# Cross-attention on one core: V's two halves as one stationary operand, and a context that is summed on VectorE and split on GpSimd

## The reference

```
q = jnp.einsum('bsd,dhk->bshk', query_input, Wq)
k = jnp.einsum('bsd,dhk->bshk', key_input, Wk)
v = jnp.einsum('bsd,dhk->bshk', value_input, Wv)
q = q * depth ** (-0.5)
logits = jnp.einsum('bthk,bfhk->bhft', k, q)
weights = jax.nn.softmax(logits, axis=-1)
ctx = jnp.einsum('bhft,bthk->bfhk', weights, v)
return jnp.einsum('bfhk,hkd->bfd', ctx, Wo)
```

## Time and profile before

| | |
|---|---|
| median of 3 runs | 3175.88 us (3175.04 to 3178.29) |
| span of the profiled execution, first to last instruction | 3171.4 us |
| PE busy | 3088.7 us, 97% of the span |
| PEld busy | 2900.2 us, 91% |
| DVE busy | 2256.1 us, 71% |
| ACT busy | 2142.4 us, 68% |
| POOL busy | 1581.9 us, 50% |
| mean granted TensorE clock | 0.990 |

### The profile page before, as it was taken

One profiled execution on the slowest core, in us unless ns is written; L12 is line 12 of the kernel. 1 busy time (PEld: TensorE's weight loads), 2 busy tenths in 40 slices (PEclk: granted clock), 3 DMA queues, 4 the chain that ended last, 5 costly groups with the idle time before them and its releaser, 6 DMA issues. The chain is left out here.

```text
span 3171.4 us, 78666 instructions
## 1 busy us (share of the span) xinstructions
PE 3088.7 (97%) x22624; PEld 2900.2 (91%) x22624; DVE 2256.1 (71%) x6566; ACT 2142.4 (68%) x6930; POOL 1581.9 (50%) x2904
## 2 busy tenths in 40 slices
PE   6999999999999998999999999999989999999998
PEld 5999999999999987999999999999868888889998
DVE  6777777777877877778877778787745455544665
ACT  6888888888887877787877877777734444442222
POOL 3666766766676765333333333333446666653000
PEclk8999999999999999999999999999989999999999
DMA  6444444444444440121111111111245444533333
GB/s 181 117 120 125 127 125 121 121 120 122 127 111 111 125 143 24 48 64 45 54 55 45 57 55 44 64 45 48 94 118 119 100 98 101 128 56 85 120 124 106
DMA packets 193684, 300.70 MB, mean 95 GB/s; under 512 B 33856, under 2 KB 134080, under 8 KB 192704
## 3 DMA queue, kind: packets, MB, share of 16 engines
q1 hardware_dynamic: 168768, 262.91, 27.8%
q0 software_dynamic: 24576, 33.57, 6.2%
HBM read 116.02 MB, written 67.11 MB: 58 GB/s over the span
## 5 line engine op out<-in xcount | busy, mean ns | idle before, releaser
L964 POOL TENSOR_SCALAR ca_prob<-ca_prob,ca_inverse 128x120 f32<-128x120 f32 x1024 | 354.6, 365 | 632.5 <-DVE ca_inverse L1268 630.5
L665 ACT ACTIVATE sa_prob<-sa_prob,sa_shift 128x128 f32<-128x128 f32 (+1 forms) x1024 | 453.6, 461 | 2.6 <-DVE sa_shift L718 2.6
L1206 ACT ACTIVATE ca_prob<-bank,ca_shift 128x120 f32<-128x120 f32 x1024 | 353.7, 366 | 6.0 <-DVE ca_shift L1262 3.5
L460 POOL TENSOR_SCALAR sa_prob<-sa_prob,sa_inverse 128x128 f32<-128x128 f32 x512 | 198.5, 388 | 234.5 <-DVE sa_inverse L726 220.4
L718 DVE CUSTOM_DVE_ANT_0 sa_prob<-bank,sa_mask 128x128 f32<-128x128 f32 (+1 forms) x1024 | 304.7, 352 | 6.9 <-PE bank L138 2.7
L136 PE MATMUL bank<-sa_ow,sa_y_hi 128*128 128x256 f32 x1024 | 279.6, 304 | 0.0
L136 PE MATMUL bank<-sa_kvT_a,sa_q 128*128 128x128 f32 (+1 forms) x1024 | 251.7, 281 | 17.7 <-DMA sa_q<-sa_q_tile 17.4
L138 PE MATMUL bank<-sa_kvT_b,sa_q 112*128 112x128 f32 (+1 forms) x1024 | 261.6, 281 | 0.0
L749 DVE TENSOR_TENSOR sa_pT_lo<-bank,sa_pT_hi 128x384 fp32r<-128x384 f32 x512 | 258.3, 544 | 1.8 <-ACT sa_pT_hi L650 1.8
L138 PE MATMUL bank<-sa_ow,sa_y_lo 112*128 112x256 f32 x1024 | 258.8, 283 | 0.0
L462 POOL TENSOR_SCALAR sa_prob<-sa_prob,sa_inverse 128x256 f32<-128x256 f32 x512 | 244.9, 478 | 0.0
(11 more groups left out here) (259 smaller groups left out, 12014.1 us busy)
## 6 DMA issues: line engine op xcount, KB each, us to landing
sa_q<-sa_q_tile SPq DMA_DIRECT2D x128, 288.0 KB
sa_q<-sa_q_tile SPq DMA_DIRECT2D x160, 112.0 KB
mid_x2T<-ca_x2T SPq DMA_DIRECT2D x32, 512.0 KB, 3.0
ex_sx<-mid_x2T SPq DMA_DIRECT2D x32, 512.0 KB, 3.3
sa_q<-sa_q_tile SPq DMA_DIRECT2D x304, 32.0 KB, 3.0
sa_xT_raw<-in_xT SPq DMA_DIRECT2D x32, 256.0 KB, 2.8
sa_q<-sa_q_tile SPq DMA_DIRECT2D x32, 256.0 KB
sa_x_res<-in_x SPq DMA_DIRECT2D x32, 256.0 KB, 2.8
```

Source lines behind the costliest of these rows:

```text
L460: pool.tensor_scalar(prob[:, r, hh, 0:P], prob[:, r, hh, 0:P], inverse[:, r, 2 * hh:2 * hh + 1], 1.0, ALU.mult, ALU.mult)
L665: act.activation(prob[:, r, hh, cols], prob[:, r, hh, cols], ACT.Exp, bias=shift[:, r, n:n + 1], scale=-1.0, accum_out=total[:, r, n:n + 1 ...
L964: ins = pool.tensor_scalar(prob[:, r, t, hh], prob[:, r, t, hh], inverse[:, r, n:n + 1], 1.0, ALU.mult, ALU.mult)
L1206: act.activation(prob[:, r, t, hh], SC[g % 2][:, n * S:n * S + S], ACT.Exp, bias=shift[:, r, n:n + 1], accum_out=total[:, r, n:n + 1]).the ...
```

## The change

`v_hi` and `v_lo` become one tensor `v`, in which each head pair has four blocks of 64 columns: high of head 0, low of head 0, low of head 1, high of head 1. A head's stationary operand is its two blocks side by side. It is multiplied by `pT_hi` and by `pT_lo`, two matmuls a head and four a step, into 256 columns of CX for each head, so all 512. The two matmuls give, for head 0, the sum with V's high part on partitions 0 to 63 and with its low part on 64 to 127; for head 1 the other way round. The product of the two low parts is now included.

ACT copies all 512 columns of CX to `cx` (SBUF). DVE adds the half that the copy holds to the half that it reads from the bank, one instruction of 64 partitions a head, into `c`; both halves read the bank at the other half's partitions. GpSimd makes `c_hi` and `c_lo` from `c`. The blocks of zeros in V, their two memsets and the wait for them are gone, and V's split takes one instruction an engine for half a sequence instead of two.

```diff
@@
-    v_hi, v_lo = al.split("v", [S, 2, NP, 3 * DH])
+    al.sb("v_before", [P, PAST_LOW])
+    cx = al.sb("cx", [P, 2, 2 * T])
+    al.sb("v_between", [P, 4 * T - PAST_LOW])
+    v = al.sb("v", [S, 2, NP, 4, DH], F32R)
...
+    c = al.sb("c", [P, 2, T])
@@ gpsimd
-            zeros = [k_hi[0:DH, :, :, S:2 * S], k_lo[0:DH, :, :, S:2 * S], k_hi[DH:P, :, :, 0:S], k_lo[DH:P, :, :, 0:S],
-                     v_hi[:, :, :, DH:2 * DH], v_lo[:, :, :, DH:2 * DH]]
+            zeros = [k_hi[0:DH, :, :, S:2 * S], k_lo[0:DH, :, :, S:2 * S], k_hi[DH:P, :, :, 0:S], k_lo[DH:P, :, :, 0:S]]
...
                 ins.then_inc(p_done, 1)
+            g = m - CL
+            if step_exists(J, g):
+                r = g % RING
+                need(pool, o_mm, upto(J, g - RING))
+                need_alone(pool, csum_done, upto(J, g, 2), spare_pool)
+                pool.tensor_scalar(c_hi[:, r], c[:, g % 2], 1.0, 1.0, ALU.mult, ALU.mult).then_inc(chalf_hi, 1)
+                need(pool, chalf_hi, upto(J, g))
+                pool.tensor_tensor(c_lo[:, r], c[:, g % 2], f32(c_hi[:, r]), ALU.subtract).then_inc(chalf_lo, 1)
@@ tensor
                 need(pe, pTlo_done, upto(J, g))
-                need(pe, cxlo_done, upto(J, g - 1))
+                need(pe, csum_done, upto(J, g - 1, 2))
                 for hh in range(2):
-                    win = slice(hh * DH, hh * DH + 2 * DH)
-                    mm = three(pe, CX[:, 0:T], v_hi[:, b, p, win], v_lo[:, b, p, win], pT_hi[:, r, hh], pT_lo[:, r, hh],
-                               hh == 0, hh == 1)
+                    both = v[:, b, p, 2 * hh:2 * hh + 2].rearrange("s a k -> s (a k)")
+                    out = CX[:, hh * T:(hh + 1) * T]
+                    pe.matmul(out, both, pT_hi[:, r, hh], start=True, stop=False, skip_group_check=True)
+                    mm = pe.matmul(out, both, pT_lo[:, r, hh], start=False, stop=True, skip_group_check=True)
                 mm.then_inc(cx_mm, 1)
...
-                need(pe, cxlo_done, upto(J, g))
+                need(pe, chalf_lo, upto(J, g))
@@ scalar
-                for hh in range(2):
-                    ins = act.activation(v_hi[:, b % 2, n * NP // 2:(n + 1) * NP // 2, hh * 2 * DH:hh * 2 * DH + DH],
-                                         v_bank(J, b, n)[0:S, :].rearrange("s (p h k) -> s p h k", h=2, k=DH)[:, :, hh], ACT.Copy)
-                ins.then_inc(vhi_done, 1)
+                act.activation(v[:, b % 2, n * NP // 2:(n + 1) * NP // 2, 0:4:3],
+                               v_bank(J, b, n)[0:S, :].rearrange("s (p h k) -> s p h k", h=2, k=DH), ACT.Copy).then_inc(vhi_done, 1)
...
-                r = g % RING
                 need(act, cx_mm, upto(J, g))
-                need(act, o_mm, upto(J, g - RING))
-                act.activation(c_hi[:, r], CX[:, 0:T], ACT.Copy).then_inc(cxhi_done, 1)
+                need(act, csum_done, upto(J, g - 2, 2))
+                act.activation(cx[:, g % 2], CX[:], ACT.Copy).then_inc(cxcopy_done, 1)
@@ vector
-                for hh in range(2):
...
-                ins.then_inc(vlo_done, 1)
+                of = v[:, b % 2, n * NP // 2:(n + 1) * NP // 2]
+                dve.tensor_tensor(of[:, :, 1:3], v_bank(J, b, n)[0:S, :].rearrange("s (p h k) -> s p h k", h=2, k=DH),
+                                  f32(of[:, :, 0:4:3]), ALU.subtract).then_inc(vlo_done, 1)
...
-                r = g % RING
-                need(dve, cxhi_done, upto(J, g))
-                dve.tensor_tensor(c_lo[:, r], CX[:, 0:T], f32(c_hi[:, r]), ALU.subtract).then_inc(cxlo_done, 1)
+                need(dve, cxcopy_done, upto(J, g))
+                need(dve, chalf_lo, upto(J, g - 2))
+                for hh in range(2):
+                    own, other = slice(hh * DH, (hh + 1) * DH), slice((1 - hh) * DH, (2 - hh) * DH)
+                    dve.tensor_tensor(c[own, g % 2], CX[other, hh * T:(hh + 1) * T], cx[own, g % 2, hh * T:(hh + 1) * T],
+                                      ALU.add).then_inc(csum_done, 1)
```

More of the change, by code:

```diff
@@ L58 @@
 CROSS_SCALE = float(DH) ** -0.5
+PAST_LOW = 576
 Later = namedtuple("Later", "own base")
@@ L860, in cross_attention @@
     p_tr, pThi_done, pTlo_done = al.sem("p_tr"), al.sem("pThi_done"), al.sem("pTlo_done")
-    cx_mm, cxhi_done, cxlo_done = al.sem("cx_mm"), al.sem("cxhi_done"), al.sem("cxlo_done")
+    cx_mm, cxcopy_done, csum_done = al.sem("cx_mm"), al.sem("cxcopy_done"), al.sem("csum_done")
+    chalf_hi, chalf_lo = al.sem("chalf_hi"), al.sem("chalf_lo")
     st_done, mv_done, ve_done, rstd_done, x2_done = (
@@ L943, in first_values @@
                 pool.memset(f32(t), 0.0).then_inc(const, 1)
-            pool.wait_ge(const, 7)
+            pool.wait_ge(const, 5)
             for q in range(SEQS):
@@ L988, in tensor @@
     def tensor(pe):
-        first_use = {1: (cross.w_lo, KC), QL: (cross.w_lo, KC * (len(CROSS) - 1)), SL: (const, 5), QL + 1: (cross.o_read, B), CL: (const, 7),
+        first_use = {1: (cross.w_lo, KC), QL: (cross.w_lo, KC * (len(CROSS) - 1)), SL: (const, 5), QL + 1: (cross.o_read, B),
                      OL: (cross.w_lo, KC * (len(CROSS) - 1) + 1), GATE: (gate_done, 1)}
@@ L1246, in slot @@
                 need(dve, vhi_done, upto_seq(J, b, 2, n - 1))
-                for hh in range(2):
-                    at = (slice(None), b % 2, slice(n * NP // 2, (n + 1) * NP // 2), slice(hh * 2 * DH, hh * 2 * DH + DH))
-                    ins = dve.tensor_tensor(v_lo[at], v_bank(J, b, n)[0:S, :].rearrange("s (p h k) -> s p h k", h=2, k=DH)[:, :, hh],
-                                            f32(v_hi[at]), ALU.subtract)
-                ins.then_inc(vlo_done, 1)
+                of = v[:, b % 2, n * NP // 2:(n + 1) * NP // 2]
+                dve.tensor_tensor(of[:, :, 1:3], v_bank(J, b, n)[0:S, :].rearrange("s (p h k) -> s p h k", h=2, k=DH),
+                                  f32(of[:, :, 0:4:3]), ALU.subtract).then_inc(vlo_done, 1)
             if m % NP == NORM % NP and seq_exists(J, (m - NORM) // NP):
```

## The result

| | before | after |
|---|---|---|
| median of the runs, us | 3176.52 (3175.04 to 3178.29) | 3197.77 (3194.34 to 3203.27) |
| profiled execution's span, us | 3171.4 | 3192.6 |

A forecast was written before the change was run, and what follows sets the result against it. PE, 97% busy, was taken as the bound. Its 59.9 us saved, less 22 for DVE's lag and 3.5 at the start, gave 34.4: span 3137, time 3142 us with 4.5 added, range 3118 to 3172.

The forecast's parts named there:

- PE's saving: Context matmuls: four in place of six at 0.117 us each save 0.234 us a step, 59.9 us over 256 steps.
- Rival 4: Context matmuls on PE: four cost as much as six because weight loads set the pace; some 3180 us, chance 0.03.
- ACT: ACT's copy of CX, 512 columns for 256: 0.21 us more a step, 6.8 us in 32 steps, still covered.
- DVE's addition: Two held half-partition adds on DVE: 0.54 us more in a step with K, 0.64 in one without.
- Rival 3: DVE's adds across partition halves are dear, up to 1.02 us more a step: slower, 3228 us, chance 0.08.
- The walk through the unequal steps: DVE's lag behind PE in uneven cross-attention steps: 2.7 us lost in 32 steps, 22 us over 256.
- the short pair: Two full short steps, twice in 32: PE waits for the second pair of adds, 0.4 us lost.
- the K steps behind the norm: Steps with K after the normalisation, twice in 32: DVE's adds finish late for PE's next context, 0.35 us lost.
- The balance of 32 steps: Engine sums over 32 cross-attention steps: DVE would need 127.5 us and PE 127.2, so they come out level.
- Rival 2: DVE becomes the bound nearly everywhere, a fifth of its idle 27 us in 32 steps staying: 3165 us, chance 0.17.
- the cover: GpSimd's split behind prob: 2.9 us of work fits steps of 3.0 to 4.0; if not, 10 us in all.
- The ends: Beside the self-attention's tail at the start, PE's saving is worth nothing and the adds cost 1 us: 3.5 us lost.

The follow-up runs named there:

- one_add: The change with one 128-partition add in place of the two 64-partition adds, head 1's context left out: 3139.39 us, ratio 0.9895.
- before_halves: The kernel before, with c_lo subtracted in two 64-partition instructions on their own partitions instead of one of 128: 3200.33 us, ratio 1.0088.
- chosen: The change's way in steps 0, 1, 5, 6, 9, 13, 14, 15 of every 16, the old way in the others: 3166.72 us, ratio 0.9972.
- opposite: The change's way in steps 2, 3, 4, 7, 8, 10, 11, 12 of every 16, the old way in the others: 3201.32 us, ratio 1.0084.
- experiment 5: The change with a third product for each head put back, so six context products a step again: 3218.29 us, ratio 1.0137.
- tail: The change with the last two steps' splits made by ACT (c_hi) and DVE (c_lo) instead of GpSimd: 3189.60 us, ratio 1.0059.
- before_pool: The kernel before, plus a dummy 128x256 copy and subtraction on GpSimd in each step, behind prob: 3182.26 us, ratio 1.0032.
- pool_norm: The change with the normalisation of x2 moved from DVE to GpSimd: 3308.83 us, ratio 1.0417.

## Why the prediction was wrong

**PE's saving: right.** Every step that PE decides became 0.20 to 0.24 shorter. Rival 4 is out. With one add in place of two (`one_add`) 42.4 of the 59.9 us arrive up to the last maximum.

**ACT: right.** The copy takes 600 ns, and with it `one_add` holds 128.55.

**DVE's addition: right.** I said 0.54 and 0.64 more a step; the starts give 0.91 in place of 0.34 from the pair to `pT_lo`, 0.57, and 0.42 in place of 0.31 in front of it without K, 0.68 in all. The halves are held, as the `k_lo` pair said and as the Trainium skill has it (VectorE: DVE Perf Modes, "Two Vector instructions with no wait between them"): the trace agrees for both adds and for `pT_lo`, and `before_halves` shows that it needs no crossing. Rival 3 named the right side for a wrong reason: the adds are not dear, 422 ns each.

**The walk through the unequal steps: wrong, and this is the step that failed.** I priced 0.4 for the short pair, 0.35 for the K steps behind the norm and 0.6 for the routing, 2.7 us in 32 steps and 22 in all. Measured were about 1.8, 1.5 and 1.0 (each twice), 8.9 with step 16, so some 70 us in all. The second step of the short pair came out as I said, 3.46 for 3.45, but by luck: PE waits there for `q_lo` and not for the sums. Two faults in it:
- I followed one result, the sums, to the next context, found that it came in time once and late by a little the second time, and took the lag for absorbed. In the steady part PE never waits for the sums. It waits for what stands behind them in DVE's stream, `ca_x`, `k_lo`, `q_lo`, `cT_lo`, whose room I had not looked at. I had counted on 20 us of waits for `ca_c`; there are none.
- I ended the walk after two steps. The third step of the short group, with the two instructions of `ca_x`, loses the most: 4.37 instead of 3.46. DVE was busy 9.59 of the 10.15 us of these three steps before, with PE waiting for nothing, and PE was to need 9.45; with 1.8 us of adds more it could not fit. That window was there to be read.

**The balance of 32 steps misled.** 127.5 for DVE and 127.2 for PE, "level", is true only if work could be moved between steps. `chosen` against `opposite` shows that it can't: nearly the same sums, 35 us apart. Rival 2 was the nearest, but with its "fifth of the idle time" also a mean.

**GpSimd beside the steady state: the cover held, with a side effect I had priced at nothing.** PE waits 1.1 us for `prob` and never for the split, so the 0.84 us of room were enough. But `ca_x` went from 445 to 635 ns in the change, 1.5 us in 32 steps, in the very steps in which DVE is the bound. By the estimate under experiment 5 that is about half of what parts the short group from `before_halves`.

**The ends.** For the start I had 3.5 us over ten steps, and it was near: context step 10 starts at 1273.55, before at 1273.47, where ten savings would have put it 2.3 earlier, so 2.4 us are lost. The granted clock, 0.91 from 1230 to 1250 us against 1.00 before, may have its part; no run shows how much. The tail I did not price at all. The place could have been read from the code: GpSimd's gathers and the next expert's weights are issued in slots 5, 6 and 10 of the last body, and the split was put in the same queue. Behind the last maximum 9.3 us were lost in the change, of which 6.3 come back in `tail`, and 5.4 up to the last output product in `before_pool`.

In sum, with 59.9 saved: 72 lost up to the last maximum where I had 25.5, and 9 behind it where I had none.

What stays open: whether all of `before_halves` is DVE's own lateness. There ACT waits 16.2 us for the maximum and PE 7.5 us for ACT's exponentials, a loop through three engines that no run took apart. Open too are the shares of the held first half and of the slower `ca_x` in steps 2 to 4, why PE's wait in step 23 goes away, and the 3 us of the tail that `tail` leaves.

## What to carry to other kernels

Before work is moved from the full engine to one with 20% idle, lay the steps side by side: here the stretches in which the second engine was already busy for 88 to 94% of the time lost 1.0 to 1.8 us each, and the steps with room did not make it good. Follow every result that stands behind the new work in its queue, not only the new one. If the steps differ, use the new way only where there is room for it; and look at what shares the queue in the last steps, where other work begins.

## What the runs showed of the hardware

- DVE's instruction over 128 partitions and 256 columns costs 342 ns from start to start when followed by one on the same partitions, two over 64 partitions 457 and 449. Halving the partitions saves no time at all: the add takes 422 ns over 64x256 and 420 over 128x256 (`one_add`), the subtraction 420 (`before_halves`) and 421 (before).
- Some of DVE's instructions that read and write SBUF become slower where GpSimd's split lies beside them: `ca_x` 445 to 635 ns and `ca_score` 222 to 322 in the change, `cT_lo` 658 to 869 and `var_eps` 169 to 325 in `before_pool`. `ca_stats`, which also reads SBUF, keeps its time (412 and 414), and so do `q_lo` and `pT_lo`, which read PSUM. The Trainium skill (SBUF — State Buffer, "SBUF: two separate sides") has a port that the two engines share and one instruction holds to its end, for DVE's with two SBUF inputs or in a fast mode. The first four rows fit that; no run here shows the modes.
- In the last products of the change the granted clock is 0.50, the 1.2 GHz level, after PE had waited 3.4 us for GpSimd; a product then costs 0.21 us where it costs 0.12 at 2.4 GHz.
- GpSimd's `tensor_scalar` with two operands from memory took 1219 ns for 128x256 (`pool_norm`), the one with two constants 404 (the change).
